# A fused attention, MLP and convolution kernel: the MLP's strip loop written out, its transposes cut into row tiles and its layers put in another order

## The chip, the cores and the metric

The kernel runs on one core of a Trainium2 chip. The metric is the device time of one launch in microseconds (us); lower is better. The kernel before took 1953.2 us (median of 3 runs, 1952.63 to 1954.0).

## The reference

The input is x, 4 images of 48 channels, 128 x 128 pixels, in float32. Three things are computed one after the other:

```
# 1. window attention (8x8 windows, 4 heads), with residual
xf = xf + proj(softmax(q k^T * scale + bias) v)        # q, k, v of layernorm(xf)
# 2. MLP per pixel, with residual: 48 -> 192 -> 48 channels
m  = layernorm(xf) * norm2_g + norm2_b
m  = gelu(m @ fc1_w.T + fc1_b)                         # exact gelu
xf = xf + (m @ fc2_w.T + fc2_b)
# 3. inverted residual block: 1x1 conv 48 -> 288, 3x3 depthwise, 1x1 conv 288 -> 48
x  = x + bn(w2 @ relu(bn(depthwise(relu(bn(w1 @ x))))))
```

The change is in part 2 alone.

## The kernel before, in words

`attention` works on groups of four pairs of windows and writes, for each pixel, its new value and its normalised value (48 numbers each, 112 columns with padding) to the buffer `tok_mid` in device memory, pixels on partitions. `mlp` reads that, computes part 2 and writes `img_mid`, channels first. `conv` reads `img_mid` and computes part 3; its program on each engine stands in the same block behind the MLP's, and its first steps (weights, borders, first pieces of the first image) run on GpSimd beside the MLP.

The MLP goes through 64 strips (`STRIPS`), each of 1024 pixels. Every engine runs `step(j, j % 4)` from `schedule` (lines 587 to 599): strips -1 to 3 written out, strips 4 to 59 in a hardware loop of four strips a turn (`Fori`), the last five written out again. In these last ones `late` also folds the convolution's batch norm constants (`roots_on_act`, `fold_on_dve`).

One `step(j)` on each engine:

- SyncE (lines 612 to 627) loads strip j+3 (`tok_mid` into `mid`, two buffers, line 615) once strip j+1's transposes are done, then waits for strip j-1's result and stores it to `img_mid` in two transfers (line 626).
- TensorE (643 to 682) does, in this order: the transposes of strip j+1, 8 of 128 rows x 112 columns, into `ps_t` (line 651); the second layer of strip j-1, first over the 128 hidden rows of `hid` (line 661, tiles of 128 rows x 64 columns, two side by side), then over the remaining 64 (line 666, tiles of 64 x 64, four side by side); the first layer of strip j (line 680), first the 128 main hidden rows (tiles of 64 x 128, two side by side), then the remaining 64 (`rest`, tiles of 64 x 64, four side by side). A float32 matmul stands in the trace as two records, a transpose as one, so a strip has 40.
- VectorE (704 to 725) copies one half of the normalised values out of `ps_t` (line 709), then both halves of the pixel values (712, two instructions), then adds second layer and residual of strip j-1 (723, two instructions).
- ScalarE (742 to 753) copies the other half of the normalised values (746), then applies Gelu to the main rows of strip j (750, two instructions) and to the rest (753, two instructions).

`ps_t` is one buffer of two banks: TensorE's transposes of strip j+2 wait until both engines have copied strip j+1 out (lines 647, 648). In it, half k of the strip stands in bank k. The order within an engine is the written order; waits are on counting semaphores.

Of the kernel before, what the change touches and what calls it, by code (L numbers as in the profile page):

```python
# [24 lines left out]
ALU = mybir.AluOpType  # L25
ACT = mybir.ActivationFunctionType
AX_X = mybir.AxisListType.X

P = 128
B, C, H, W = 4, 48, 128, 128  # L30
WS, NH = 8, 4
HD = C // NH
NT = WS * WS
EPS = 1e-5
ONE = 64
LN_AT, X_AT = (0, ONE), (ONE, 0)
# [3 lines left out]
PAIRS = GW // (2 * WS)  # L40
# [3 lines left out]
MID = 112  # L44
# [22 lines left out]
def wait(eng, sem, n):  # L67

    if not isinstance(n, int) or n >= 1:
        eng.wait_ge(sem, n)  # L70
# [470 lines left out]
def mlp(nc, d, block, room, psum, stored, emptied, roots_on_act, fold_on_dve):  # L541
# [4 lines left out]
    with ExitStack() as ctx:  # L546
        used = [0]

        def sb(name, shape):
# [28 lines left out]
        ident_loaded = sem("m_ident")  # L578
        loaded = [sem(f"mid_loaded{s}") for s in range(2)]
        gelu_done, y_done = emptied  # L580
        turned, ln_copied, x_copied, hid_ready, y_ready = (
            sem(n) for n in ("m_turned", "m_ln_copied", "m_x_copied", "m_hid_ready", "m_y_ready"))

        def has(j):
            return not isinstance(j, int) or 0 <= j < STRIPS

        def schedule(eng, step, early=None, late=None):

            for j in range(-1, 4):
                if j == 0 and early:  # L590
                    early(eng)
                step(j, j % 4)
            with eng.Fori(4, STRIPS - 7, 4) as j:
                for t in range(4):
                    step(j + t if t else j, t)
            for j in range(STRIPS - 4, STRIPS + 1):
                if late:
                    late(eng, j - STRIPS + 4)
                step(j, j % 4)

# [30 lines left out]
        @block.tensor  # L631
        def _(pe):
            pe.wait_ge(ident_loaded, 16)

            def early(pe):
                pe.wait_ge(w_loaded, 16 * 13)
                nc.tensor.matmul(ps_y[:, 0, 0:1], fc1[0:C, 0:P], b[:, :], start=True, stop=True)
                for k in range(2):
                    mm = nc.tensor.matmul(ps_y[REST * k:REST * k + REST, 0, 1:2], fc1[0:C, P:HID0], b[:, :], start=True, stop=True)
                mm.then_inc(w_bias, 1)  # L640
                pe.wait_ge(w_ready, 2)

            def step(j, t):
                s = t % 2
                if has(j + 1):
                    pe.wait_ge(loaded[1 - s], 8 * (j + 1 - (1 - s)) + 16)
                    wait(pe, ln_copied, j + 1)
                    wait(pe, x_copied, j + 1)
                    for k in range(2):
                        for p in range(PAIRS):  # L650
                            mm = nc.tensor.transpose(ps_t[0:MID, k, P * p:P * p + P], mid[1 - s][:, k, p, :], ident[:, :])  # L651
                    mm.then_inc(turned, 1)
                if has(j - 1):
                    pe.wait_ge(gelu_done, 4 * j - 2)
                    wait(pe, y_done, j - 1)
                    at = slice(COLS * (1 - s), COLS * (1 - s) + COLS)
                    for c in range(2):
                        for k in range(2):
                            if c and k:
                                pe.wait_ge(gelu_done, 4 * j)  # L660
                            nc.tensor.matmul(ps_y[64 * k:64 * k + 64, c, at], w2[:, :],  # L661
                                             hid[1 - s][:, k, COLS * c:COLS * c + COLS], start=True, stop=False)
                    for k in range(2):
                        for c in range(2):
                            rows = slice(REST * c, REST * c + REST)
                            mm = nc.tensor.matmul(ps_y[64 * k:64 * k + 64, c, at], w2r[c][rows, :], hidr[1 - s][rows, k, :],  # L666
                                                  start=False, stop=True)
                    mm.then_inc(y_ready, 1)
                if has(j):
                    pe.wait_ge(ln_copied, j + 1)  # L670
                    pe.wait_ge(x_copied, j + 1)
                    wait(pe, gelu_done, 4 * j)
                    for rest in range(2):
                        for c in range(2):
                            cols = slice(COLS * c, COLS * c + COLS)
                            for k in range(2):
                                rows = slice(ONE * k, ONE * k + ONE)
                                dst, w = ((ps_r[k][REST * c:REST * c + REST, :], w1[rows, P:HID0]) if rest else
                                          (ps_h[:, k, cols], w1[rows, 0:P]))
                                mm = nc.tensor.matmul(dst, w, lnT[s][rows, cols], start=True, stop=True)  # L680
                                if c:
                                    mm.then_inc(hid_ready, 1)

            schedule(pe, step, early)

        @block.vector
        def _(dve):
            for t in (w1, w2, w2r[0], w2r[1]):
                nc.vector.memset(t[...], 0.0)
            nc.vector.memset(b2c[:, :], 0.0).then_inc(fixed, 1)  # L690
            for t in (*lnT, *xT, *y):
                last = nc.vector.memset(t[...], 0.0)
            last.then_inc(w_ready, 1)
            dve.wait_ge(w_loaded, 16 * 13)
            dve.wait_ge(w_ready, 1)

            def early(dve):
                for at in LN_AT:
                    nc.vector.tensor_scalar(w1[at:at + C, :], fc1[at:at + C, :], g[at:at + C, 0:1], None, ALU.mult)
                dve.wait_ge(w_bias, 1)  # L700
                nc.vector.tensor_tensor(b1[:, :], b1[:, :], ps_y[:, 0, 0:1], ALU.add)
                nc.vector.tensor_tensor(b1r[:, :], b1r[:, :], ps_y[:, 0, 1:2], ALU.add).then_inc(w_ready, 1)

            def step(j, t):
                s = t % 2
                if has(j + 1):
                    wait(dve, y_done, j - 2)
                    dve.wait_ge(turned, j + 2)
                    nc.vector.tensor_copy(lnT[1 - s][ONE:ONE + C, :], ps_t[LN_AT[1]:LN_AT[1] + C, 1, :])
                    for k in range(2):  # L710
                        r = slice(64 * k, 64 * k + C)
                        last = nc.vector.tensor_scalar(xT[(t + 1) % 4][r, :], ps_t[X_AT[k]:X_AT[k] + C, k, :], b2c[r, 0:1], None,  # L712
                                                       ALU.add)
                    last.then_inc(x_copied, 1)
                if has(j - 1):
                    dve.wait_ge(x_copied, j)
                    dve.wait_ge(y_ready, j)
                    wait(dve, stored[1 - s], 16 * (j - 1 - (1 - s)))
                    px = lambda ap: ap.rearrange("q (n r c) -> q n r c", r=WS, c=WS)
                    for c in range(2):  # L720
                        at = slice(COLS * (1 - s), COLS * (1 - s) + COLS)
                        dst = y[1 - s][:, :, 1 + GW // 2 * c:1 + GW // 2 * c + GW // 2].rearrange("q r (n c) -> q n r c", c=WS)
                        last = nc.vector.tensor_tensor(dst, px(ps_y[:, c, at]), px(xT[(t + 3) % 4][:, COLS * c:COLS * c + COLS]),
                                                       ALU.add)
                    last.then_inc(y_done, 1)

            schedule(dve, step, early, fold_on_dve)

        @block.scalar
        def _(act):  # L730
# [5 lines left out]
                act.dma_start(dst, src).then_inc(w_loaded, 16)  # L736
            act.wait_ge(w_ready, 1)

            def early(act):
                act.wait_ge(w_ready, 2)  # L740

            def step(j, t):
                s = t % 2
                if has(j + 1):
                    act.wait_ge(turned, j + 2)
                    nc.scalar.activation(lnT[1 - s][0:C, :], ps_t[LN_AT[0]:LN_AT[0] + C, 0, :], ACT.Copy).then_inc(ln_copied, 1)
                if has(j):
                    for k in range(2):
                        act.wait_ge(hid_ready, 4 * j + k + 1)
                        nc.scalar.activation(hid[s][:, k, :], ps_h[:, k, :], ACT.Gelu, bias=b1[:, 0:1]).then_inc(gelu_done, 1)  # L750
                    for k in range(2):
                        act.wait_ge(hid_ready, 4 * j + k + 3)
                        nc.scalar.activation(hidr[s][:, k, :], ps_r[k], ACT.Gelu, bias=b1r[:, 0:1]).then_inc(gelu_done, 1)

            schedule(act, step, early, roots_on_act)


def conv(nc, d):
# [590 lines left out]
```

## Time and profile before

| | |
|---|---|
| runs | 1952.63, 1953.2, 1954.0 us |
| profiled execution, span | 1952.0 us |
| TensorE matmul busy | 1870.2 us (96%) |
| TensorE weight load busy | 1565.2 us (80%) |
| VectorE busy | 1445.8 us (74%) |
| ScalarE busy | 1322.8 us (68%) |
| GpSimd busy | 647.1 us (33%) |
| MLP, from the first transpose to the last addition | 779.5 to 1073.0 us |

The profile is of one execution; its span is 1.2 us below the median of the runs. Its times count from the span's start. Matmuls are pipelined, so a busy TensorE is not one at its peak: how long a group of matmuls holds the engine is read from the start of its first weight load to the start of the next group's.

### The profile page before, as it was taken

To read this page: it belongs to the slowest core of one execution; us is meant where nothing else is said; L and a number is where in the kernel's file an instruction comes from. 1 tells how busy PE (TensorE), PEld (TensorE's weight loads), DVE (VectorE), ACT (ScalarE), POOL (GpSimd) and SP (SyncE) were. 2 spreads that over 40 slices of the span, in tenths; PEclk is the share of its full clock that TensorE was granted. 3 is DMA by queue.
4 is the path that set the end of the run, shared out by engine and by line. 5 is a ranking of instruction groups with operands and counts; after the bars stand their busy time and mean duration, and the time that the engine had idled before them with its cause. 6 is when DMAs were issued, how large, how long until landed. Compare 5 with 4: busy or idle time off the path is not lost.

```text
span 1952.0 us, 74705 instructions
## 1 busy us (share of the span) xinstructions
PE 1870.2 (96%) x29960; PEld 1565.2 (80%) x29960; DVE 1445.8 (74%) x2650; ACT 1322.8 (68%) x2838; POOL 647.1 (33%) x869
## 2 busy tenths in 40 slices
PE   5999999999999996999999999999999999999998
PEld 4888888888888885555555899999999999999997
DVE  5999999999999997666667556566566566566564
ACT  2788878878888885555555666666666666666665
POOL 4333333333333333413100434325334343344240
PEclk9999999999999998999999999999999999999999
DMA  2222222222222222777664444545363454445331
GB/s 67 68 73 76 78 73 76 77 73 76 77 72 77 74 76 77 182 171 179 161 150 111 97 108 126 99 113 126 87 147 86 112 137 102 103 129 105 99 111 34
DMA packets 286410, 198.43 MB, mean 102 GB/s; under 512 B 225991, under 2 KB 275672, under 8 KB 276504
## 3 DMA queue, kind: packets, MB, share of 16 engines
q1 hardware_dynamic: 282114, 189.12, 37.9%
q0 software_dynamic: 2368, 6.25, 1.5%
q8 instruction: 149, 2.44, 0.5%
q10 hardware_dynamic: 1750, 0.39, 0.1%
q14 instruction: 29, 0.24, 0.0%
HBM read 128.36 MB, written 54.72 MB: 94 GB/s over the span
## 4 chain that ended last, share of the span: by engine, by line
PE 56%; ACT 2%; DMA 1%; issue 1%; DVE 0%; SPq 0%; ACTq 0%; DVEq 0%
PE psum L1126 14%; PE psum L1145 13%; PE psum L1171 9%; PE psum L1180 5%; PE psum L680 5%; PE psum L661 3%; PE psum L651 3%; PE psum L666 2%; ACT h2T L1227 1%; DMA room<-tok_mid 1%; ACT h L884 1%; DMA room<-in_ident 0%; ACT room L750 0%; DVE room L885 0%; DVE room L712 0%
## 5 line engine op out<-in xcount | busy, mean ns | idle before, releaser
L934 POOL TENSOR_TENSOR mats<-mats,dscale 112x2048 f32<-112x2048 f32 x72 | 260.8, 3622 | 315.0 <-DMA mats<-in_taps 312.6
L1126 PE MATMUL psum<-ew,xp 64*100 64x96 f32 x6144 | 322.4, 252 | 16.8 <-ACT h L884 13.5
L885 DVE TENSOR_SCALAR h<-psum 100x384 f32<-100x384 f32 x384 | 211.9, 557 | 151.7 <-PE psum L1126 141.6
L1126 PEld LDWEIGHTS psum<-ew,xp 64*100 64x100 f32 x6144 | 295.5, 165 | 26.3 <-ACT h L884 18.6
L1227 ACT ACTIVATE h2T<-psum 96x1024 f32<-96x1024 f32 x192 | 195.6, 1019 | 177.5 <-PE psum L1180 177.5
L1145 PE MATMUL psum<-h,mats 101*64 101x128 f32 x4608 | 269.2, 274 | 1.6 <-issue 0.9
L1145 PEld LDWEIGHTS psum<-h,mats 101*64 101x64 f32 x4608 | 252.0, 137 | 11.8 <-issue 2.0
L884 ACT ACTIVATE room<-psum 64x512 f32<-64x512 f32 (+1 forms) x384 | 206.1, 537 | 78.1 <-PE psum L1145 71.5
L344 PE MATMUL psum<-kb,qa 128*64 128x256 f32 x2048 | 244.0, 380 | 0.8 <-DVE prob L443 0.8
L885 DVE TENSOR_SCALAR room<-psum 64x512 f32<-64x512 f32 (+1 forms) x288 | 174.2, 605 | 64.7 <-PE psum L1145 58.8
L884 ACT ACTIVATE h<-psum 100x384 f32<-100x384 f32 x384 | 186.6, 486 | 48.1 <-PE psum L1126 34.1
L1171 PE MATMUL psum<-h2T,pw 128*64 128x128 f32 x3072 | 195.0, 277 | 10.1 <-ACT h2T L1227 9.4
L344 PEld LDWEIGHTS psum<-kb,qa 128*64 128x64 f32 x2048 | 140.6, 138 | 56.3 <-issue 1.9
L1171 PEld LDWEIGHTS psum<-h2T,pw 128*64 128x64 f32 x3072 | 167.6, 137 | 21.4 <-ACT h2T L1227 13.7
L526 POOL TENSOR_TENSOR xn<-cen,rstd 128x192 f32<-128x192 f32 x128 | 64.9, 507 | 339.6 <-ACT rstd L499 339.6
L750 ACT ACTIVATE room<-psum,room 128x512 f32<-128x512 f32 x128 | 81.1, 686 | 120.3 <-PE psum L680 120.3
L436 DVE TENSOR_REDUCE top<-psum 128x16 f32<-128x1024 f32 x128 | 156.7, 1224 | 7.1 <-PE psum L344 4.7
L443 DVE TENSOR_TENSOR prob<-psum,top 128x1024 f32<-128x1024 f32 x128 | 155.8, 1217 | 0.1
L471 ACT ACTIVATE probT<-psum 128x512 f32<-128x512 f32 x256 | 151.2, 601 | 0.0
L908 POOL COPY xp<-piece 128x400 f32<-128x400 f32 x128 | 67.6, 528 | 241.5 <-DMA piece<-img_mid 223.3
L396 PE MATMUL psum<-vb,probT 128*64 128x26 f32 x4096 | 143.4, 219 | 1.6 <-issue 1.0
L396 PEld LDWEIGHTS psum<-vb,probT 128*64 128x64 f32 x4096 | 129.9, 138 | 18.6 <-issue 1.2
(154 smaller groups left out, 3228.3 us busy)
## 6 DMA issues: line engine op xcount, KB each, us to landing
mats<-in_taps SPq DMA_DIRECT2D x69, 896.0 KB, 5.9
tok_mid<-mid SPq DMA_DIRECT2D x128, 224.0 KB, 1.9
room<-tok_mid SPq DMA_DIRECT2D x64, 448.0 KB, 4.4
piece<-img_mid SPq DMA_DIRECT2D x196, 63.8 KB, 2.4
img_mid<-room SPq DMA_DIRECT2D x128, 97.5 KB, 3.0
kb<-kk SPq DMA_DIRECT2D x512, 24.0 KB
out<-yc SPq DMA_DIRECT2D x32, 384.0 KB, 4.5
scratch<-in_x_tokens SPq DMA_DIRECT2D x126, 96.0 KB, 1.9
```

The costliest lines, as they stand in the source:

```text
L344: mm = nc.tensor.matmul(ps_s[NT * w:NT * w + NT, p // 2, 256 * (p % 2):256 * (p % 2) + 256], qa[s][:, NT * n:NT * n + NT], kb[s][:, n, :, ...
L396: mm = nc.tensor.matmul(ps_o[NT * w:NT * w + NT, at:at + 2 * VE], probT[:, p, h, NT * w:NT * w + NT], vb[1 - s][:, p, h, w, :], start=True ...
L436: nc.vector.tensor_reduce(top[s][:, :], sc, AX_X, ALU.max).then_inc(top_done, 1)
L443: nc.vector.tensor_tensor(prob[s][:, :, :], sc, bc(top[s][:, :], 2, NT), ALU.subtract)\
L471: nc.scalar.activation(probT[:, 2 * k:2 * k + 2, :, :].rearrange("q p h n -> q (p h n)"), ps_p[:, k, :], ACT.Copy)\
L884: return nc.scalar.activation(dst, src, ACT.Relu)
L885: return nc.vector.tensor_scalar(dst, src, 0.0, None, ALU.max)
L934: nc.gpsimd.tensor_tensor(m, m, bc(scale[0:MROWS, at:at + TCH], 2, POUT), ALU.mult).then_inc(mats_scaled, 1)
L1126: mm = nc.tensor.matmul(ring[(j + u) % 4][0:PIN, p:4 * CH:4], xp[hx][rows, 2 * j + p, :], w1[rows, c, :], start=True, stop=True)
L1145: mm = nc.tensor.matmul(bank[:, n % 4:4 * PATCHES:4], mats[ch // TCH][0:PIN + 1, ch % TCH, :], h1[0:PIN + 1, ch, :], start=True, stop=True)
L1171: mm = nc.tensor.matmul(ps_y[n % 2][64 * r:64 * r + 64, at:at + PCOLS], w2[:, c, :], h2T[n % 2][:, r, at:at + PCOLS], start=True, stop=True)
L1227: nc.scalar.activation(h2T[n % 2][0:CH, :, :], turned_at(n, last)[0:CH, :, 0:POUT * PART], ACT.Copy).then_inc(copied, 1)
```

## The change

Three things, all in `mlp`:

1. `schedule` has no hardware loop any more. All 66 steps are written out on every engine. (The `early` parts move into the steps, to the same place.)
2. A strip's transposes are 16 row tiles instead of 8 full ones: `mid`'s rows 0 to 63 and 64 to 127 are turned apart, each against a 64 x 64 part of the identity. The upper rows' results go to bank 0 of `ps_t`, the lower rows' to bank 1, so a half of the strip is now spread over both banks, and the copies of ScalarE and VectorE read runs of 64 elements from the two banks in turn (`turned_part`, `by_half`).
3. TensorE's order within step j becomes: transposes of j+1, main part of the first layer of j, second layer of j-1, `rest` part of the first layer of j+1. ScalarE's becomes: copy of j+1, Gelu of the main part of j, Gelu of the rest of j+1. VectorE's second copy of pixel values waits for ScalarE's copy.

```diff
-        def schedule(eng, step, early=None, late=None):
-            for j in range(-1, 4):
-                if j == 0 and early:
-                    early(eng)
-                step(j, j % 4)
-            with eng.Fori(4, STRIPS - 7, 4) as j:
-                for t in range(4):
-                    step(j + t if t else j, t)
-            for j in range(STRIPS - 4, STRIPS + 1):
-                if late:
+        def turned_part(rows, k):
+            return ps_t[rows, :, TOK // 2 * k:TOK // 2 * k + TOK // 2].rearrange("q e (p t) -> q p e t", t=NT)
+        def by_half(t):
+            return t.rearrange("q (p e t) -> q p e t", e=2, t=NT)
+        def gelus_of_rest(j):
+            return 4 * j + 2
+        def gelus_of_main(j):
+            return 4 * j + 4
+        def schedule(eng, step, late=None):
+            for j in range(-1, STRIPS + 1):
+                if late and j >= STRIPS - 4:
                     late(eng, j - STRIPS + 4)
                 step(j, j % 4)
...  (TensorE, step)
                         for p in range(PAIRS):
-                            mm = nc.tensor.transpose(ps_t[0:MID, k, P * p:P * p + P], mid[1 - s][:, k, p, :], ident[:, :])
+                            at = NT * (PAIRS * k + p)
+                            for e in range(2):
+                                rows = slice(NT * e, NT * e + NT)
+                                mm = nc.tensor.transpose(ps_t[0:MID, e, at:at + NT], mid[1 - s][rows, k, p, :], ident[rows, rows])
                     mm.then_inc(turned, 1)
+                if j < 0:
+                    early(pe)
+                if has(j):
+                    wait(pe, gelu_done, gelus_of_main(j - 1))
+                    for c in range(2):
+                        cols = slice(COLS * c, COLS * c + COLS)
+                        for k in range(2):
+                            rows = slice(ONE * k, ONE * k + ONE)
+                            mm = nc.tensor.matmul(ps_h[:, k, cols], w1[rows, 0:P], lnT[s][rows, cols], start=True, stop=True)
+                            if c:
+                                mm.then_inc(hid_ready, 1)
                 if has(j - 1):
-                    pe.wait_ge(gelu_done, 4 * j - 2)
+                    pe.wait_ge(gelu_done, gelus_of_main(j - 1))
                     wait(pe, y_done, j - 1)
...
-                            if c and k:
-                                pe.wait_ge(gelu_done, 4 * j)
...
+                rest(j + 1, 1 - s)
+            def rest(j, s):
                 if has(j):
                     pe.wait_ge(ln_copied, j + 1)
-                    pe.wait_ge(x_copied, j + 1)
-                    wait(pe, gelu_done, 4 * j)
-                    (both parts of the first layer, main and rest)
+                    pe.wait_ge(ln1_copied, j + 1)
+                    wait(pe, gelu_done, gelus_of_rest(j - 1))
+                    for c in range(2):
+                        cols = slice(COLS * c, COLS * c + COLS)
+                        for k in range(2):
+                            rows = slice(ONE * k, ONE * k + ONE)
+                            mm = nc.tensor.matmul(ps_r[k][REST * c:REST * c + REST, :], w1[rows, P:HID0], lnT[s][rows, cols],
+                                                  start=True, stop=True)
+                            if c:
+                                mm.then_inc(hid_ready, 1)
...  (VectorE)
-                    nc.vector.tensor_copy(lnT[1 - s][ONE:ONE + C, :], ps_t[LN_AT[1]:LN_AT[1] + C, 1, :])
+                    nc.vector.tensor_copy(by_half(lnT[1 - s][ONE:ONE + C, :]), turned_part(slice(LN_AT[1], LN_AT[1] + C), 1))\
+                        .then_inc(ln1_copied, 1)
                     for k in range(2):
+                        if k:
+                            dve.wait_ge(ln_copied, j + 2)
...  (ScalarE)
+                if j < 0:
+                    act.wait_ge(w_ready, 2)
                 if has(j):
                     for k in range(2):
-                        act.wait_ge(hid_ready, 4 * j + k + 1)
+                        act.wait_ge(hid_ready, 4 * j + 2 + k + 1)
                         nc.scalar.activation(hid[s][:, k, :], ps_h[:, k, :], ACT.Gelu, bias=b1[:, 0:1]).then_inc(gelu_done, 1)
+                if has(j + 1):
                     for k in range(2):
-                        act.wait_ge(hid_ready, 4 * j + k + 3)
-                        nc.scalar.activation(hidr[s][:, k, :], ps_r[k], ACT.Gelu, bias=b1r[:, 0:1]).then_inc(gelu_done, 1)
+                        act.wait_ge(hid_ready, 4 * (j + 1) + k + 1)
+                        nc.scalar.activation(hidr[1 - s][:, k, :], ps_r[k], ACT.Gelu, bias=b1r[:, 0:1]).then_inc(gelu_done, 1)
```

## Rows read from the trace of the kernel before

**Rows 1.** Windows: length, busy of PE, PEld, DVE, ACT, POOL, clock, DMA share, GB/s.

```profile
850.00:950.00 100.00, 99.61 (x914) 57.30 (x912) 66.78 (x115) 55.78 (x114) 29.28 (x53) 1.00 0.77 177
950.00:1046.00 96.00, 96.00 (x878) 55.26 (x879) 64.97 (x110) 53.59 (x111) 0.00 (x0) 1.00 0.63 150
```

**Rows 2.** Timeline of one MLP strip, TensorE's weight loads: start, length, instructions.

```profile
905.03 0.84 PEld L651 LDWEIGHTS psum<-room 128*112 128x112 f32 x8 [0.39 <-issue]
...
906.05 0.73 PEld L661 LDWEIGHTS psum<-room 128*64 128x64 f32 x8 [0.18 <-ACT room L750]
...
907.16 0.21 PEld L666 LDWEIGHTS psum<-room 64*64 64x64 f32 x8 [0.38 <-issue]
...
907.75 0.73 PEld L680 LDWEIGHTS psum<-room 64*128 64x128 f32 x8 [0.39 <-issue]
...
908.82 0.21 PEld L680 LDWEIGHTS psum<-room 64*64 64x64 f32 x8 [0.33 <-issue]
...
909.41 0.84 PEld L651 LDWEIGHTS psum<-room 128*112 128x112 f32 x8 [0.39 <-issue]
```

**Rows 3.** Timeline of the same strip, the other engines.

```profile
906.15 0.70 DVE L709 COPY room<-psum 48x512 f32<-48x512 f32 x1 [1.36 <-PE psum L651]
...
906.30 0.41 SPq L615 DMA_DIRECT2D room<-tok_mid  x1
906.41 0.59 ACT L746 ACTIVATE room<-psum 48x512 f32<-48x512 f32 x1
...
906.87 1.52 DVE L712 TENSOR_SCALAR room<-psum,room 48x512 f32<-48x512 f32 x2
...
908.41 0.75 DVE L723 TENSOR_TENSOR room<-psum,room 128x256 f32<-128x256 f32 x2
...
908.92 1.27 ACT L750 ACTIVATE room<-psum,room 128x512 f32<-128x512 f32 x2 [1.93 <-PE psum L680]
909.33 0.83 SPq L626 DMA_DIRECT2D img_mid<-room  x2
...
910.08 0.84 ACT L753 ACTIVATE room<-psum,room 128x256 f32<-128x256 f32 x2
```

**Rows 4.** Timeline of TensorE in the convolution, between 1500 and 1506 us.

```profile
1501.38 0.61 PE L1180 MATMUL psum<-ident,room 64*96 64x64 f32 x16
1501.83 1.61 PE L1126 MATMUL psum<-ew,xp 64*100 64x96 f32 x32
1503.36 1.97 PE L1171 MATMUL psum<-h2T,pw 128*64 128x128 f32 x32
1505.26 0.65 PE L1180 MATMUL psum<-ident,room 64*96 64x64 f32 x16
1505.75 1.70 PE L1126 MATMUL psum<-ew,xp 64*100 64x96 f32 x32
```

**Rows 5.** Lines of copies by form: count, busy us, mean ns, idle before.

```profile
L453 DVE COPY qa<-psum 48x512 f32<-48x512 f32 x128 | 87.5, 684 | 11.6 <-PE psum L384 7.7
```

**Rows 6.** Line 615's loads, issue to landing, at 860 to 950, then 950 to 1046 us.

```profile
DMA to landing us min/median/max: 4.4/4.9/5.4
...
DMA to landing us min/median/max: 3.9/4.2/4.4
```

**Rows 7.** The chain that ended last, MLP: two pieces that are loads.

```profile
816.78 9.05 DMA room<-tok_mid
...
844.57 7.92 DMA room<-tok_mid
```

**Rows 8.** Timeline, first and last strips of the MLP.

```profile
789.11 0.84 PEld L651 LDWEIGHTS psum<-room 128*112 128x112 f32 x8 [0.41 <-issue]
...
1049.68 0.84 PEld L651 LDWEIGHTS psum<-room 128*112 128x112 f32 x8 [0.39 <-issue]
...
1072.22 0.76 DVE L723 TENSOR_TENSOR room<-psum,room 128x256 f32<-128x256 f32 x2 [1.75 <-issue]
```

**Rows 9.** The page, DMA queue of instructions: packets, MB, share of 16 engines.

```profile
q8 instruction: 149, 2.44, 0.5%
```

More of the change, by code:

```diff
@@ L580, in mlp @@
         gelu_done, y_done = emptied
-        turned, ln_copied, x_copied, hid_ready, y_ready = (
-            sem(n) for n in ("m_turned", "m_ln_copied", "m_x_copied", "m_hid_ready", "m_y_ready"))
+        turned, ln_copied, ln1_copied, x_copied, hid_ready, y_ready = (
+            sem(n) for n in ("m_turned", "m_ln_copied", "m_ln1_copied", "m_x_copied", "m_hid_ready", "m_y_ready"))
+        def turned_part(rows, k):
[6 more added lines that the diff above has]
+            return 4 * j + 4
         def has(j):
             return not isinstance(j, int) or 0 <= j < STRIPS
-        def schedule(eng, step, early=None, late=None):
-            for j in range(-1, 4):
-                if j == 0 and early:
-                    early(eng)
-                step(j, j % 4)
-            with eng.Fori(4, STRIPS - 7, 4) as j:
-                for t in range(4):
-                    step(j + t if t else j, t)
-            for j in range(STRIPS - 4, STRIPS + 1):
-                if late:
+        def schedule(eng, step, late=None):
+            for j in range(-1, STRIPS + 1):
+                if late and j >= STRIPS - 4:
                     late(eng, j - STRIPS + 4)
@@ L668, in step @@
                     mm.then_inc(y_ready, 1)
+                rest(j + 1, 1 - s)
+            def rest(j, s):
                 if has(j):
                     pe.wait_ge(ln_copied, j + 1)
-                    pe.wait_ge(x_copied, j + 1)
-                    wait(pe, gelu_done, 4 * j)
[L673 to L684, printed above, removed]
+                    pe.wait_ge(ln1_copied, j + 1)
[8 more added lines that the diff above has]
+                                mm.then_inc(hid_ready, 1)
+            schedule(pe, step)
         @block.vector
@@ L708, in step @@
                     dve.wait_ge(turned, j + 2)
-                    nc.vector.tensor_copy(lnT[1 - s][ONE:ONE + C, :], ps_t[LN_AT[1]:LN_AT[1] + C, 1, :])
+                    nc.vector.tensor_copy(by_half(lnT[1 - s][ONE:ONE + C, :]), turned_part(slice(LN_AT[1], LN_AT[1] + C), 1))\
+                        .then_inc(ln1_copied, 1)
                     for k in range(2):
+                        if k:
+                            dve.wait_ge(ln_copied, j + 2)
                         r = slice(64 * k, 64 * k + C)
-                        last = nc.vector.tensor_scalar(xT[(t + 1) % 4][r, :], ps_t[X_AT[k]:X_AT[k] + C, k, :], b2c[r, 0:1], None,
-                                                       ALU.add)
+                        last = nc.vector.tensor_scalar(by_half(xT[(t + 1) % 4][r, :]), turned_part(slice(X_AT[k], X_AT[k] + C), k),
+                                                       b2c[r, 0:1], None, ALU.add)
                     last.then_inc(x_copied, 1)
+                if j < 0:
+                    early(dve)
                 if has(j - 1):
@@ L725, in step @@
                     last.then_inc(y_done, 1)
-            schedule(dve, step, early, fold_on_dve)
+            schedule(dve, step, fold_on_dve)
         @block.scalar
@@ L737, in _ @@
             act.wait_ge(w_ready, 1)
-            def early(act):
-                act.wait_ge(w_ready, 2)
             def step(j, t):
@@ L745, in step @@
                     act.wait_ge(turned, j + 2)
-                    nc.scalar.activation(lnT[1 - s][0:C, :], ps_t[LN_AT[0]:LN_AT[0] + C, 0, :], ACT.Copy).then_inc(ln_copied, 1)
+                    nc.scalar.activation(by_half(lnT[1 - s][0:C, :]), turned_part(slice(LN_AT[0], LN_AT[0] + C), 0), ACT.Copy)\
+                        .then_inc(ln_copied, 1)
+                if j < 0:
+                    act.wait_ge(w_ready, 2)
                 if has(j):
                     for k in range(2):
-                        act.wait_ge(hid_ready, 4 * j + k + 1)
+                        act.wait_ge(hid_ready, 4 * j + 2 + k + 1)
                         nc.scalar.activation(hid[s][:, k, :], ps_h[:, k, :], ACT.Gelu, bias=b1[:, 0:1]).then_inc(gelu_done, 1)
+                if has(j + 1):
                     for k in range(2):
-                        act.wait_ge(hid_ready, 4 * j + k + 3)
-                        nc.scalar.activation(hidr[s][:, k, :], ps_r[k], ACT.Gelu, bias=b1r[:, 0:1]).then_inc(gelu_done, 1)
-            schedule(act, step, early, roots_on_act)
+                        act.wait_ge(hid_ready, 4 * (j + 1) + k + 1)
+                        nc.scalar.activation(hidr[1 - s][:, k, :], ps_r[k], ACT.Gelu, bias=b1r[:, 0:1]).then_inc(gelu_done, 1)
+            schedule(act, step, roots_on_act)
 def conv(nc, d):
```

## The prediction

> **What bounds the kernel now.** First the windows over the MLP: between 950 and 1046 us TensorE is busy for 96.00 of 96.00 us at a granted clock of 1.00, VectorE for 65 and ScalarE for 54 [rows 1]. 878 matmul records at 40 a strip are 22 strips, 4.38 us each, five returns of the hardware loop among them, and no return leaves a gap. So the stage goes at TensorE's pace, and what counts is how long TensorE is held per strip. For that, the timeline of one strip [rows 2]: what a group costs is the distance from its first weight load to the next group's. Transposes 905.03 to 906.05: 1.02. Second layer, main: 1.11. Second layer, rest: 0.59. First layer, main: 1.07. First layer, rest: 0.59. Together 4.38.
>
> **What such a stretch consists of.** Count the columns that pass: transposes 8 x 128 = 1024; second layer main, 8 records of 256 columns two at a time = 1024; each of the rests, 8 records of 256 four at a time = 512; first layer main 1024. A stretch of 1024 takes 1.02 and one of 512 takes 0.59 [rows 2]: that is 0.43 us per 512 columns and 0.16 per stretch. The 0.16 fits the idle time of 0.33 to 0.39 that every group's weight loads have before them. The five groups have five different neighbours in tile shape (128x128, 128x64, 64x64, 64x128, 64x64). The convolution shows a stretch with no change of shape: 16 transposes of 64x96, 8 x 64 = 512 columns, start at 1501.38, and matmuls of 64x100, the same 64x128 tile, follow at 1501.83: 0.45. Behind matmuls of 128x64 the same transposes take 0.49 (1505.26 to 1505.75), and these matmuls, 2048 columns, take 1.90 = 4 x 0.43 + 0.18 [rows 4]. So a change of tile shape costs some 0.16, and neighbours of one shape cost nothing. Check on the strip: 4096 columns are 3.44, five changes 0.80, sum 4.24. The 0.14 missing is in the two stretches over 1.02: the second layer, whose last main matmul waits for ScalarE's Gelu, and the first layer with its 128-column weights.
>
> **The change, part by part.**
>
> *Transposes in row tiles.* 512 columns for 1024: 0.45 to 0.49 from the convolution's rows for 96 columns of weights. Here they are 112. Bounds: 0.45, or, if the stretch grows with the weights, 0.57. I take 0.49, since the convolution's stretch is just what its moving columns need. Gain 0.53.
>
> *Order.* The new order is transposes, first layer main (both 64x128), second layer main (128x64), second layer rest, first layer rest (both 64x64). Three changes stand for five: 2 x 0.16 = 0.32 less (bounds 0.2 and 0.4). The second layer's main part no longer waits inside for Gelu of the strip just done, at most 0.09. Sum by stretches: transposes 0.49, first layer main 1.04, second layer main 1.03, second layer rest 0.43, first layer rest 0.59, less 0.06 for the change in the transposes' 0.49 that the 0.59 holds already = 3.52 us per strip, bounds 3.45 and 3.65. Against 4.38 that is 0.86.
>
> *Do the other engines keep up?* VectorE has 0.70 + 1.52 + 0.75 = 2.97, ScalarE 0.59 + 1.27 + 0.84 = 2.70 [rows 3], both under 3.52. The chain that returns: transposes end, copies start 1.12 after the transposes' first load today (0.10 after their end), so 0.6 to 0.7 in the new step; 2.22 of copies end at 2.9; the next transposes come at 3.52. 0.6 spare. VectorE's addition waits for the second layer, which ends at 0.49 + 1.04 + 1.03 + 0.43 = 2.99 and is seen near 3.15; it ends at 3.9, and the next copy comes at 4.2. ScalarE: rest Gelus from 0.05 to 0.9, copy to 1.5, main Gelus to 2.8, and TensorE needs those no sooner than the next first layer at 4.0. The new wait of VectorE's second pixel copy (at 2.1) is for ScalarE's copy (done at 1.5); behind it on VectorE stand that copy, for which the next transposes wait, and the addition. It costs nothing in the steady strips.
>
> *Reading two banks in runs of 64.* The row nearest to it is the attention's copy of 48x512 that alternates between two banks in runs of 128: 0.684 [rows 5] against 0.697 for the straight copy [rows 3]. Zero, bounds 0 and, at 20% on the three, 0.45, which the 0.6 spare still covers.
>
> *Loop written out.* No return costs anything now, so nothing is gained. The Trainium skill (Runtime: NRT & Kernel Launch, Instruction fetch mechanics) says that a taken branch outside the fetched window costs a stall and full unrolling avoids it; by it the change would gain some more. The trace does not agree: no gap in 96 us with five returns [rows 1].
>
> *SyncE.* The issues of a strip take 0.41 and 0.83 [rows 3]. The order in this queue is load, then wait for the addition, then two stores, and the next load stands behind those. Today the load goes 1.27 after the transposes begin, on their end, and has 2 x 4.38 - 1.27 = 7.5 us until it is needed. After: additions end at 3.9, stores are issued by 4.9, so the load goes 1.4 into the next step and has 2 x 3.52 - 1.4 = 5.6. It lands after 4.4 to 5.4 while GpSimd's pieces run beside it, and after 3.9 to 4.4 later [rows 6]. It just fits. Two loads do not: those beside the convolution's filters took 9.05 and 7.92 [rows 7]. They will be late by 3.4 and 2.3, where they cost some 2.0 before (below); with 1 us for others that lands at 6.7, thus 4.7 more.
>
> *First and last strips.* At the head the first transposes are shorter: 0.5 gain (an estimate, about one strip's saving on them; bounds 0 and 1). In the tail, from 1049.68 to the last addition's end at 1072.98 [rows 8], 23.3 us pass where undisturbed strips would take some 17: the batch norm constants on ScalarE and VectorE set the time there. Those constants stay as they are, and the new wait puts VectorE's copy behind ScalarE's roots once. Bounds: 20 and 25; I take 23, as today, so no gain.
>
> **Sum.** From the transposes at 789.11 to those at 1049.68 [rows 8] are 59 strips in 260.6 us: 258.6 of strips and 2.0 of late loads. After: 59 x 3.52 = 207.7, plus 6.7 = 214.4. Gain 46.2, with the head 0.5 about 46.7. The profiled execution would go from 1952.0 to 1905.3, and the median, 1.2 above it, from 1953.2 to 1906.5. The convolution behind starts earlier by as much and keeps its length: GpSimd cuts its first pieces beside the MLP, with work between 850 and 950 us and none after [rows 1], and the MLP would end at some 1026.
>
> **The rivals.**
>
> *Loads become the limit.* The 16 DMA engines have a share of 0.63 at 4.38 us a strip, and 0.77 with the pieces [rows 1]. At 3.52 these are 0.78 and some 0.93. If landing rises from 4.9 to 7 there, two strips take 1.4 + 7 = 8.4, so 4.2 a strip; over the 26 strips beside the pieces up to 18 us are lost: 1925. At half of that 1916. For: the shares. Against: with 0.77 the landing is only 0.7 above that with 0.63 [rows 6], and late loads ease their own crowding.
>
> *Copies become the limit.* The Trainium skill (TensorEngine Tiling (Array Packing), PSUM Bottleneck) warns that tiling speeds up TensorE but not the emptying of PSUM, which may become the bottleneck. Here that means: if the two-bank reads cost more than 0.2 us each, the chain from transposes over VectorE to the next transposes is longer than 3.52. At +0.3 on the three it is 3.8, 59 x 0.28 = 16.5 less: 1923. Against it the 0.684 [rows 5]; the trace so far has VectorE busy for 68% of the stage [rows 1].
>
> *The row tiles don't run side by side.* The 16 transposes then take 0.95 as the 8 do now: 59 x 0.46 = 27, 1934. Against: the convolution's [rows 4].
>
> *Slower: code comes late.* Written out, TensorE passes a 16 KB packet of code every 2.5 strips or so, some 24 in all. A packet takes 0.005 x 16 x 1952 / 149 = 1.0 us [rows 9] on an engine that is not otherwise loaded. If each were asked for only when needed, and queued behind strip data, at more than 46.7 / 24 = 1.9 us each the gain is gone; at 3 us the time is 1979. Against: the convolution is written out and its groups follow without gaps [rows 4].
>
> **Chances.** Forecast 0.66 (its own range 1899 to 1913), loads 0.17, copies 0.06, transposes 0.04, code 0.03, anything else that saves less 0.04. The range from 3.45 with no more late loads than now (59 x 0.93 + 0.5 = 55, so 1898) to the loads' full case short of its end: 1898 to 1921. A measurement tells 0.2% (4 us) from no change; only the code case reaches there: faster 0.96, same 0.01, slower 0.03.
>
> **What would show it.** Starts of weight loads some 3.5 apart from strip to strip; transposes to first layer main within 0.5; no idle time before the first layer's rest, and three idle times a strip on the weight loads; waits of line 651's successor on loads near the filters, of 3 and 2 us. A VectorE copy over 0.8, a landing over 5.6 throughout, or loads of weights waiting for "issue" by a microsecond would show the rivals. The prediction is wrong if strips take over 3.7, or if the tail is longer than 25.

## The result and the profile after

The changed kernel took 1928.7 us (median of 4 runs, 1923.87 to 1930.64) against 1953.13. The ratio is estimated at 0.9866, 95% interval 0.9852 to 0.988; the quotient of the two medians, 0.9875, lies within it. The kernel is faster by 24.4 us where 46.7 were forecast, and 1928.7 lies outside the range of 1898 to 1921. Run again beside other kernels it took 1928.25.

How long an undisturbed strip takes is told by the timeline of one strip, TensorE's weight loads. It answers to [rows 2].

```profile
972.44 0.52 PEld L661 LDWEIGHTS psum<-room 64*112 64x112 f32 x16 [0.82 <-DMA room<-tok_mid]
...
972.89 0.73 PEld L671 LDWEIGHTS psum<-room 64*128 64x128 f32 x8
...
973.95 0.63 PEld L680 LDWEIGHTS psum<-room 128*64 128x64 f32 x8 [0.33 <-issue]
...
974.97 0.21 PEld L685 LDWEIGHTS psum<-room 64*64 64x64 f32 x8 [0.39 <-issue]
...
975.24 0.37 PEld L699 LDWEIGHTS psum<-room 64*64 64x64 f32 x8
...
975.99 0.52 PEld L661 LDWEIGHTS psum<-room 64*112 64x112 f32 x16 [0.39 <-issue]
```

Transposes to transposes is 3.55 us where 3.52 was forecast. Transposes 0.45, first layer main 1.06, second layer main 1.02, the two rests together 1.02. Three of the five groups have an idle time before them. The first layer's main part (L671) directly behind the transposes has none, nor has its rest (L699) behind the second layer's rest: those are the neighbours of one tile shape. But the transposes at 972.44 have 0.82 of idle before them, and it ends with a load of a strip.

The windows over the stage answer to [rows 1]: in the stretch with GpSimd's pieces TensorE is busy for 92.21 of 100 us, and from 975 to 1020 us for 43.45 of 45.00.

```profile
850.00:950.00 100.00, 92.21 (x1218) 54.18 (x1216) 74.61 (x127) 66.12 (x126) 22.68 (x38) 0.98 0.87 190
...
975.00:1020.00 45.00, 43.45 (x590) 25.92 (x592) 35.93 (x61) 31.68 (x61) 0.00 (x0) 1.00 0.79 178
```

What it waits for stands in the list of waits between 785 and 1045 us (who waited for whom; us in total, times, longest):

```profile
PEld psum L661 <- DMA room<-tok_mid: 33.7, 35, 4.8
...
PE psum L661 <- DMA room<-tok_mid: 18.0, 18, 4.4
...
DVE room L748 <- DMA img_mid<-room: 6.5, 3, 3.7
```

35 of 64 transposes' weight loads waited for a strip. (33.7 holds the idle time of the change of shape too; 18.0 is what the matmuls lost.) The loads' times from issue to landing, at 860 to 950 and at 950 to 1020 us, answer to [rows 6]; there it was 4.9 and 4.2 in the middle:

```profile
DMA to landing us min/median/max: 4.9/5.8/6.9
...
DMA to landing us min/median/max: 5.0/5.8/6.5
```

The two profiled executions compare like this. Times are in us, from the first matmul of each strip's transposes:

| | before | after | gain |
|---|---|---|---|
| 59 strips undisturbed | 59 x 4.383 = 258.6 | 59 x 3.552 = 209.6 | 49.0 |
| their delays | 2.0 | 24.8 | -22.8 |
| start of the 59 strips | 789.1 | 789.7 | -0.5 |
| from there to the last addition | 23.3 | 22.2 | 1.1 |
| behind the MLP | 879.0 | 875.5 | 3.5 |
| span | 1952.0 | 1921.7 | 30.3 |

The delays are not spread evenly. The 16 strips that begin before 860 us, beside GpSimd's weight and filter loads, lose 15.6 us; the 23 up to 950 us lose 6.7, and the 20 behind lose 2.4.

This profiled execution is the shortest of the four runs: the median gained 24.4, and the changed kernel's other profiled execution had a span of 1926.8 with a mean strip of 4.05, so delays of some 29.5.

### The profile page after: what moved, and what is told of

Same layout as the page of the kernel before. It is cut to its first block, busy times and chain, and to the rows that moved or that the text cites. A ratio compares the mean times of both kernels' runs of the same rounds, so it can differ in the third digit from the quotient of the medians.

```text
span 1921.7 us, 74758 instructions
## 1 busy us (share of the span) xinstructions
PE 1822.4 (95%) x30472; PEld 1540.3 (80%) x30472; DVE 1446.4 (75%) x2650; ACT 1333.8 (69%) x2838; POOL 648.1 (34%) x869
## 4 chain that ended last, share of the span: by engine, by line
PE 48%; DMA 6%; ACT 2%; DVE 2%; issue 1%; SPq 1%; ACTq 0%; DVEq 0%
PE psum L1152 14%; PE psum L1171 14%; PE psum L1197 10%; DMA room<-tok_mid 5%; PE psum L1206 5%; PE psum L671 2%; PE psum L680 2%; ACT h2T L1253 1%; PE psum L661 1%; DVE room L748 1%; PE psum L685 1%; SPq L633 1%; DVE room L735 1%; ACT h L910 1%; PE psum L699 0%
## 5 line engine op out<-in xcount | busy, mean ns | idle before, releaser
L1253 ACT ACTIVATE h2T<-psum 96x1024 f32<-96x1024 f32 x192 | 195.8, 1020 | 175.2 <-PE psum L1206 175.2
L511 ACT ACTIVATE prob<-prob 128x1024 f32<-128x1024 f32 x128 | 135.3, 1057 | 4.6 <-DVE prob L443 1.6
```

The source lines that it names most:

```text
L1253: nc.scalar.activation(h2T[n % 2][0:CH, :, :], turned_at(n, last)[0:CH, :, 0:POUT * PART], ACT.Copy).then_inc(copied, 1)
```

## Experiments

The theory: an undisturbed strip is as short as forecast, and what is missing is lost because a strip's load is issued too late for the time it takes to land. In undisturbed strips the load is issued 1.41 us after the transposes begin, so 2 x 3.55 - 1.41 = 5.7 us ahead of its use, and it lands after 5.8. The rival: the DMA engines can't carry a strip's bytes in 3.55 us. Both are late loads; they differ in what a longer lead does. Strip lengths below are distances between the first transposes of neighbouring strips, mean over strips 2 to 60, from each kernel's profiled execution. The kernels ran on several chips; each ratio is to the kernel before on the same chip.

| kernel | time, us | ratio (95%) | undisturbed strip | mean strip |
|---|---|---|---|---|
| before | 1953.1 | 1 | 4.38 | 4.42 |
| changed | 1928.7 | 0.9866 (0.9852 to 0.988) | 3.55 | 3.97 |
| third read buffer | 1910.3 | 0.977 (0.9746 to 0.9794) | 3.55 | 3.73 |
| load ahead of the store | 1922.3 | 0.984 (0.9824 to 0.9857) | 3.55 | 3.93 |
| both | 1921.0 | 0.983 (0.9814 to 0.9847) | 3.55 | 3.89 |
| GpSimd's loads held back | 1983.3, one run | | 3.55 | 3.73 |
| three read, three write buffers | 1903.7 | 0.9744 (0.9727 to 0.976) | 3.55 | 3.59 |
| the same, filter loads in parts | 1903.3 | 0.9733 (0.9717 to 0.975) | 3.55 | 3.59 |
| changed, filter loads in parts | 1921.6 | 0.9826 (0.981 to 0.9843) | 3.55 | 3.98 |
| before, loop written out | 1953.2 | 0.9995 (0.9986 to 1.0005) | 4.38 | 4.42 |
| the same, row-tile transposes | 1951.3 | 0.9985 (0.9975 to 0.9995) | 4.38 | 4.39 |
| changed, full transposes | 1943.3 | 0.9943 (0.9926 to 0.9959) | 4.12 | 4.29 |

**A third buffer for the strips read.**

```diff
-        mid = [sb(f"midb{s}", [P, 2, PAIRS, MID]) for s in range(2)]
+        mid = [sb(f"midb{s}", [P, 2, PAIRS, MID]) for s in range(3)]
-                    wait(sp, turned, j - 1)
+                    wait(sp, turned, j - 2)
-                load(j + 3, 1 - s)
+                load(j + 4, (j + 4) % 3)
```

> The changed kernel with a third buffer for the strips, so that a load goes out a strip earlier (9.2 us ahead of its use instead of 5.7). Theory (the loads are late because they are issued too late for a landing of 5.9 us): undisturbed and mean strip both about 3.55 us, waits of the transposes on loads under 3 us in all, no dips of the clock, 59 x (3.97 - 3.58) = 23 us under the changed kernel: 1904 us, 1899 to 1910. Rival (the DMA engines can't move a strip in 3.55 us with what runs beside it): landing grows with the lead, mean strip stays near 3.9, 1920 to 1930 us.

1910.3 us, 0.3 over the theory's range. Of the transposes' waits on loads one is left, of 0.6 us, though loads now land after 6.5 us in the middle beside the pieces. One dip of the clock is left too (at 829.89 us), where none was expected. The mean strip stays at 3.73, and another transfer comes late in a few places, the stores. Its list of waits:

```profile
DVE room L748 <- DMA img_mid<-room: 15.5, 7, 4.2
...
PE psum L680 <- DVE room L748: 6.4, 6, 2.4
```

**The load ahead of the store** in SyncE's queue, with two read buffers and with three.

```diff
-                if has(j - 1):
-                    sp.wait_ge(y_done, j)
+                if has(j - 2):
+                    sp.wait_ge(y_done, j - 1)
...              (stores strip j-2 instead of j-1)
```

> The changed kernel with the store of a strip put behind the next load in SyncE's queue, nothing else moved: the load is issued on the end of the transposes, 0.7 us earlier, and the stores' packets are no longer right ahead of it in the rings. Theory (late issue, stores in front): landing falls from 5.9 to 4.5 to 5, lead 6.4, so loads are late only beside the filters: 1906 us, 1902 to 1914. Rival (throughput): the same bytes in the same time, 1920 to 1930 us. A second rival, that a store now later holds up VectorE's addition, would show as waits of VectorE on stores and 1915 or more.

> Third strip buffer and load ahead of the store together. Theory: like the third buffer alone, since its lead of 9.2 us already covers all but the filters' landings (up to 10.3): 1902 us, 1898 to 1908. Rival (throughput): 1920 or more.

Both missed their main forecast; of the first, the second rival that was written down came, waits of VectorE on stores and 1915 or more. The load's landing fell from 5.8 to 5.5 us at 860 to 950, and the store's rose from 4.4 to 5.8; then VectorE waited for stores 42 times (46 with three read buffers):

```profile
DVE room L749 <- DMA img_mid<-room: 45.3, 42, 3.7
...
PEld psum L662 <- DMA room<-tok_mid: 2.7, 5, 0.7
```

The wait moved from one side to the other: the transfer that was put ahead landed sooner and the other one later. That load and store slow each other down in flight is a reading of this, and no run has one without the other. The rule of the Trainium skill that on each DMA engine descriptors are consumed in ring order (DMA: Bandwidth & Descriptors, Queues, rings and completion order) fits it. Whether separate queues would help was not tried.

**GpSimd's loads held back** until the MLP is over.

```diff
+            pool.wait_ge(mlp_done, STRIPS)
             for s in range(LOADS - 1):
-                pool.wait_ge(mlp_done, 6 * (s + 1))
```

> The changed kernel with GpSimd's filter and piece loads held back until the MLP is over, so that strips have the DMA engines alone; the convolution starts later, so only the strips' lengths count, not the time. Theory (lead too short by itself): loads still land after 5.6 to 5.9 us, the mean strip is about 3.72 as in the changed kernel's stretch without pieces (975 to 1020 us), and no wait is over 1 us. Rival (it is what GpSimd moves that makes loads late): landing back to 4.2, every strip 3.55.

The time is long since the convolution starts late; only the strips count. At 860 to 950 us only the strips' own loads and stores are on the DMA engines, and loads still land after 5.6 us in the middle, and 42 weight loads of transposes still end a wait on a load, up to 2.5 us, more than the 1 us that was expected. The mean strip is 3.73. So of the 0.42 us that a strip of the changed kernel loses on average, 0.18 is there without the filters' and pieces' loads and the other 0.24 comes with them. The rows are the list of waits and the loads' landing at 860 to 950 us:

```profile
PEld psum L661 <- DMA room<-tok_mid: 26.7, 42, 2.5
...
DMA to landing us min/median/max: 4.6/5.6/7.0
```

**Three buffers on both sides**, then the filters' loads in parts.

```diff
-        y = [sb(f"y{s}", [P, WS, GW + 2]) for s in range(2)]
+        y = [sb(f"y{s}", [P, WS, GW + 2]) for s in range(3)]
-        xT = [sb(f"xT{s}", [P, TOK]) for s in range(4)]
+        xT = [sb(f"xT{s}", [P, TOK]) for s in range(3)]
...      (with the third read buffer; store semaphores one for each of the three)
-                pool.wait_ge(mlp_done, 6 * (s + 1))
-                pool.dma_start(mats[s][0:MROWS, :, :], d["taps"][s]).then_inc(mats_begun[s], 16)
+                for q4 in range(4):
+                    pool.wait_ge(mlp_done, 4 + 6 * s + q4)
+                    part = slice(TCH // 4 * q4, TCH // 4 * (q4 + 1))
+                    pool.dma_start(mats[s][0:MROWS, part, :], d["taps"][s][:, part, :]).then_inc(mats_begun[s], 16)
```

> The changed kernel with three buffers for the strips read and three for the strips written (the pixel values' buffers go from four to three to make room). With the third read buffer alone the transposes no longer waited for loads but VectorE's addition waited 15.5 us in 7 places for stores. Theory (lead on both sides was all that was missing, the DMA engines have the throughput): mean strip 3.60, 1904 us, 1900 to 1909. Rival (throughput): waits move again and the mean stays at 3.73: 1910 or more.

> The same with GpSimd's two 896 KB filter loads each cut into four parts, one a strip, from strips 4 and 10 on. Theory (a filter load shuts the strips out for up to 10 us): no strip over 5 us beside the filters, no dip of the clock, 3 to 6 us under the kernel with three buffers each: 1900 us. Rival (the buffers already cover it): same as that one within 1.5 us.

> The changed kernel with its two buffers, filter loads in four parts each. [...] Theory: 5 to 8 us of these come back: 1922. Rival (same bytes, same lateness): 1928.

> The changed kernel again, on the same chip as its versions with more buffers. Both theories: 1924 to 1931 us, mean strip 3.9 to 4.0. If it came out near 1910 the differences between these kernels would be those of the chip.

Three buffers on both sides: 1903.7 us, as expected, and 56 of its 59 strips take 3.55. Its ratio (0.9727 to 0.976) and that of the third read buffer alone (0.9746 to 0.9794) overlap at their ends; the mean strips, 3.59 and 3.73, are 8 us apart over 59. With the filters in parts nothing is gained on top (1903.3, where 1900 was expected), and its rival came: the buffers already cover them. Windows of the kernel with three buffers beside the pieces and at their end:

```profile
850.00:950.00 100.00, 100.00 (x1366) 60.06 (x1364) 83.22 (x142) 72.64 (x142) 24.41 (x41) 1.00 0.94 204
950.00:1000.00 50.00, 50.00 (x678) 30.01 (x678) 41.50 (x71) 36.36 (x72) 4.86 (x12) 1.00 0.92 196
```

TensorE is busy for all of both at a DMA share of 0.94 and 204 GB/s, more than the changed kernel moved with its waits (0.87, 190). Beside the filter loads, from 805 to 850 us, it is busy for 43.09 of 45.00 at a share of 1.00. Its loads land after 6.4 us in the middle, later than those of the changed kernel:

```profile
DMA to landing us min/median/max: 5.8/6.4/7.8
```

So the rival falls from 850 us on: the bytes can be carried in 3.55 us a strip. What was missing was lead, 5.7 us for loads and its like for stores. In two buffers the filters in parts gave 1921.6 against 1928.3 of the changed kernel on the same chip, where 1922 was expected. In its profiled execution the strips before 860 us lose 9.8 us where those of the changed kernel lost 15.6 and 16.4, and the 7.99 + 4.98 and 5.95 + 5.16 us of the strips beside the two filter loads are gone; but the strips behind 860 us lose 15.6 where those lost 9.1 and 13.0, so the mean strip of 3.98 does not tell it from the changed kernel. The changed kernel, run again, came within its range (1928.25); its mean strip of 4.05 was just over it.

**The parts of the change alone.** Loop written out on the kernel before; on top of it the row tiles with their copies; and the changed kernel with the full transposes.

```diff
 before, loop written out:  -  with eng.Fori(4, STRIPS - 7, 4) as j: ...
                            +  for j in range(-1, STRIPS + 1): ...
 row tiles:                 +  the change's 16 transposes, turned_part, by_half, the wait on ln_copied
 changed, full transposes:  -  the change's 16 transposes, turned_part, by_half
```

> The kernel before with the MLP's loop written out and nothing else. Theory (loop returns cost nothing and code comes in time): within 2 us of before, strips of 4.38. Rival (code fetched beside the strips costs): gaps before weight loads once in 2.5 strips, 1960 or more. Rival (a taken branch costs): up to 10 us faster.

> The kernel before, loop written out, with row-tile transposes and their copies alone, TensorE's order as before (five changes of tile shape). By the prediction's columns an undisturbed strip is 512 columns shorter: 4.38 - 0.43 = 3.95, and with a lead of 2 x 3.95 - 1.4 = 6.5 us the loads are in time: 59 x 0.43 = 25 us less, 1928, which is as fast as the changed kernel. Rival (tiles don't run side by side): 1953.

> The changed kernel with full transposes of 128 rows and straight copies: order alone. By the prediction four changes of shape stand for five and the wait on Gelu inside the second layer is gone: 4.38 - 0.16 - 0.09 = 4.13, loads in time: 1938, 1934 to 1944. If changes of shape cost nothing here, 1948 (only the wait gone).

Writing the loop out does nothing to the time (0.9995). It may do something to the transfers: with strips of 4.38 us as before, loads land after 5.3 us at 860 to 950 and 4.7 at 950 to 1020, where the kernel before had 4.9 and 4.2 [rows 6], stores after 4.0 for 3.2, and the DMA share is 0.82 for 0.77 [rows 1]. The rows are its window at 850 to 950 and its two landings:

```profile
850.00:950.00 100.00, 99.19 (x908) 57.18 (x906) 66.36 (x114) 56.30 (x115) 24.40 (x41) 1.00 0.82 172
...
DMA to landing us min/median/max: 4.3/5.3/7.2
...
DMA to landing us min/median/max: 4.5/4.7/5.4
```

The version with the row tiles on top has the same (5.4 and 4.6). These are one profiled execution each and perhaps of another chip than that of the kernel before, so the loop as the cause is not shown.

The new order alone gives strips of 4.12 us where 4.13 was expected; in its time 5 us are lost again, 1943.3 against 1938, with a mean strip of 4.29: 9.1 us of delays before 860 us and 0.1 behind. The row tiles alone missed by nearly all of their 25 us: strips stay at 4.38, and 1951.3 is near the rival's 1953. The rival's reason is not the cause: 16 row tiles' weights load in 0.53 us, where the 8 full ones took 0.84 [rows 2]. The timeline shows why:

```profile
984.92 1.27 ACT L758 ACTIVATE room<-psum,room 128x512 f32<-128x512 f32 x2 [1.93 <-PE psum L686]
985.41 0.53 PEld L657 LDWEIGHTS psum<-room 64*112 64x112 f32 x16 [0.39 <-issue]
...
986.07 0.84 ACT L761 ACTIVATE room<-psum,room 128x256 f32<-128x256 f32 x2
...
986.24 1.38 PE L667 MATMUL psum<-room 128*64 128x256 f32 x8 [0.17 <-ACT room L758]
...
987.54 0.21 PEld L672 LDWEIGHTS psum<-room 64*64 64x64 f32 x8 [0.39 <-issue]
988.13 0.73 PEld L686 LDWEIGHTS psum<-room 64*128 64x128 f32 x8 [0.39 <-issue]
...
989.30 1.27 ACT L758 ACTIVATE room<-psum,room 128x512 f32<-128x512 f32 x2 [1.93 <-PE psum L686]
```

In the old order a circle runs through both engines. First layer's weight loads at 988.13, Gelu from 989.30, both pairs of Gelu 1.99 long (984.92 to 986.91), and only then the last main matmul of the second layer, behind which the next first layer comes: 984.92 to 989.30 is 4.38 again. The transposes got shorter (985.41 to 986.24, with a wait on Gelu in it), and the second layer's main part takes 1.30 where it took 1.11 [rows 2]. The kernel before ran in the same circle. There both pairs of Gelu take 1.99 too:

```profile
904.54 1.27 ACT L750 ACTIVATE room<-psum,room 128x512 f32<-128x512 f32 x2 [1.93 <-PE psum L680]
...
905.69 0.84 ACT L753 ACTIVATE room<-psum,room 128x256 f32<-128x256 f32 x2
```

They end at 906.53, and from there the second layer's rest begins 0.63 later (907.16), the next first layer another 0.59 (907.75) and Gelu another 1.17 (908.92) [rows 2, rows 3]. With row tiles the same steps are 0.63, 0.59 and 1.17 (986.91, 987.54, 988.13, 989.30). So it was the circle that gave 4.38 in both, and TensorE's own work was a little shorter: by an estimate at most 4.28, the 4.12 of the new order with full transposes and one change of shape more. The new order puts the transposes and the next first layer ahead of the second, which cuts the circle.

## Why the prediction was wrong

Point by point, by its own steps:

- *What bounds the kernel: TensorE's time a strip.* Wrong, without harm. A circle through ScalarE's Gelu set the 4.38, and TensorE's own work was some 0.1 shorter; the trace shows TensorE busy throughout all the same. The 0.18 of idle before the second layer, ended by ScalarE, in [rows 2] hinted at it, and the prediction put that wait at 0.09 at most. It made no difference to the forecast, since the order and the tiles came together: that was luck. Alone, the tiles' 0.53 would have been wrong.
- *Transposes in row tiles, 0.49; three changes of shape; 3.52 a strip.* Right: 0.45, three idle times, 3.55.
- *Other engines keep up.* Right in the steady strips: VectorE's copies take 0.70 and 1.52 as before, from two banks too. TensorE's transposes waited for them at two places, 1.1 us in all. The Trainium skill's warning on PSUM (TensorEngine Tiling (Array Packing), PSUM Bottleneck) did not come true: VectorE at 2.97 us of work still fits in 3.55.

```profile
973.21 0.70 DVE L729 COPY room<-psum 48x512 f32<-48x512 f32 x1 [0.68 <-PE psum L661]
973.43 0.55 SPq L622 DMA_DIRECT2D room<-tok_mid  x1
973.94 1.52 DVE L735 TENSOR_SCALAR room<-psum,room 48x512 f32<-48x512 f32 x2
```

- *Loop written out, nothing.* Right for the time, by experiment; the landings may have grown with it. The Trainium skill's rule on taken branches (Runtime: NRT & Kernel Launch, Instruction fetch mechanics) has no part in the time here: 0.9995.
- *SyncE: the load has a lead of 5.6 and lands after 4.4 to 5.4, "it just fits".* This step failed. The lead was right (5.7), the landing was not. It was read off the kernel before, with strips of 4.38 us, and taken to hold at 3.52. It measured 5.8 in the middle in both stretches, and 5.6 even without GpSimd's filters and pieces. The way there in the runs: 4.9 before, 5.3 with the loop written out at 4.38, 5.6 with the new order at 4.12, 5.8 in the changed kernel at 3.55 (at 950 to 1020 us 4.2, 4.7, 5.1, 5.8). So it rises where the same two transfers follow each other more closely, but part of the rise was there with the strips as long as before, and why is open. The term "6.7 for late loads" measured 24.8. Of these 9.1 are lost from 860 us on, where 1 us was allowed for all others. Before 860 us the two strips that wait beside the filter loads lost 4.4 and 2.4, near the 3.4 and 2.3 of the sum; a third one, behind loads of the convolution's weights, lost 2.9, and the strips behind these three some 4 in all to a lower clock (last section), a cost that the prediction did not have.
- *First and last strips, behind the MLP.* Small: -0.5 for 0.5, 1.1 for 0, 3.5 for 0. The 3.5 is not understood; the kernel before with only its loop written out has 875.7 us there too, for 879.0, without a gain in its median time.
- *The rival "loads become the limit".* It came, and a bit beyond its full price (1925; 1928.7). But it was written down as a matter of shares, for the 26 strips beside the pieces only, and with a chance of 0.17. The lateness is in all stretches, and it is a matter of lead: at a share of 0.94 with three buffers nothing waits from 850 us on. That its price came so near is luck in part: it had 18 us for the strips beside the pieces, and the profiled execution lost 6.7 there. With a lead only 0.2 us over the longest landing seen, a transfer that lands a little later deserved more than 0.17.

## What to carry to other kernels

When a strip got shorter here, the lead of its loads and stores shrank with it while their landing got longer. Take a landing time read from the slower kernel as a floor, so if it only just fits, count on waits and deepen the buffers in the same change, for stores as well as for loads: here a third buffer on both sides gave back 25 us, some 18 of them on the side of the loads. And shortening one engine's work pays only after the circles of waits through other engines have been measured: against the kernel before on the same chip, the tiles alone gave 3 us, the order alone 11, both with enough buffers 51.

## What the hardware showed beyond that

The longest waits of TensorE were followed by a lower clock. After 4.37 us without a matmul, at 827.19, the granted clock was 0.51 for 3.4 us, its lower level (1.2 GHz), and the transposes' weight loads took 0.91 instead of 0.52. The rows are two of the changed kernel's timeline and its window over that stretch:

```profile
827.18 0.91 PEld L661 LDWEIGHTS psum<-room 64*112 64x112 f32 x16 [4.82 <-DMA room<-tok_mid]
827.19 1.10 PE L661 MATMUL psum<-room 64*112 64x64 f32 x16 [4.37 <-DMA room<-tok_mid]
```

```profile
826.80:830.20 3.40, 3.01 (x26) 2.19 (x28) 1.75 (x3) 0.66 (x2) 0.00 (x0) 0.51 0.66 137
```

The strip behind took 4.98 for 3.55. The profiled execution has three such dips in the MLP, beginning at 802.95, 826.85 and 854.15 us, each about where TensorE had been without a matmul for 2.9, 4.4 and 2.3 us. The strips behind took 4.95, 4.98 and 5.16, so some 4 of the 24.8 us are clock, an estimate from 3 x 3.55. Not every such wait had a dip: in the kernel with the load ahead of the store one of 2.54 us at 853.64 had none. The kernel before had none in the MLP behind its first strips, nor had the one with three buffers on both sides.
